# Spreading a three-hop graph kernel's softmax over its gather steps and moving all of its dense rows beside the first hop's scatters

## The chip, the cores and the metric

The kernel runs on one core of one Trainium2 chip. The metric is the device time of one execution in microseconds (us), lower is better. TensorE is called PE, VectorE DVE, ScalarE ACT, GpSimd POOL, and SyncE SP; SP computes nothing here and issues most of the DMAs.

## The reference

There are 50,000 rows of 128 floats (`x`), and 25,000 edges with a source row (`head`, in the code's terms), a destination row (`tail`) and one of 64 types. `h` is the layer norm of `x` with a ReLU. Three times ("hops") this is done, starting from `agg = h`:

```
left = agg[head] @ q_w;  right = tanh((rel * agg[tail]) @ k_w);  att = sum(left * right, axis=1)
w = softmax of att over the edges that have the same head
agg = segment_sum(w * rel * agg[tail], head) / max(count, 1), then each row divided by its norm
out = out + agg + h
```

The result is `x + out`. Rows that are no edge's head have an aggregate of zero, so for them the result is `x + 3 h`. That is the "dense part": it is done for all rows, and the rows that have edges are overwritten at the end.

## The kernel before, in words

The kernel first sorts the edges by head. Then it works on 200 tiles of 125 edges, in 50 groups of 4 tiles (`NG`, `GT`), and the groups form four chunks of 13, 13, 13 and 11 groups (`GC`). Each hop has the same shape.

**Gather steps.** POOL issues one indirect DMA for each tile of a group (`fetch`, L599; in hop 0 two, for tail and head) into a ring of `TS` = 5 groups. For each group DVE multiplies the gathered rows with the relation rows (`product`, L1065), PE transposes (`turn`, L1351), multiplies with `kw` (`keys`, L1358) and with `qw` (`back`, L1371 and L1373), ACT copies and takes the tanh, and DVE forms the scores three steps later (`scores`, L1088). Hop 0 has 29 steps of two groups (a few of one), and a layer norm in each; hops 1 and 2 have 53 steps of one group. A ring place is free for the next fetch once `product` has run, and in hop 0 also once the row that was gathered for the head has been stored to `acc_d`.

**Softmax of a chunk.** When the scores of a chunk are there (steps in `SOFT_AT`), DVE runs `softmax(h, b)` in one piece: seven times it asks PE for a small transpose, or ACT for the exponential, and waits for the answer (`to_pe`, L951 to L971). PE then multiplies each tile with its weights for the rows that cross from tile to tile (`parts`, L1399), `PARTS` tiles a step, and `carries` gives the carried rows to SP, which writes them into `rt` (`s_cy`).

**Sums.** For a group j of a finished chunk, DVE makes the weights (`weights`, L1003), PE forms the segment sums (L1416), ACT squares and copies them (L1239, L1241), and six groups later DVE scales them (`scale`, L1023; in hop 2 L1029 to L1033, with three rows from memory that SP loads with `load_last`). Every fifth group there is `norms` (L1011 to L1018). During the gather steps a sum is done in each step (in hop 2 every other step) as soon as chunks are ready; what is left runs behind the last gather step, after the softmax of the last chunk: groups 17 to 49 in hop 0, 32 to 49 in hop 1, 16 to 49 in hop 2.

**Between the hops.** After the gathers of hop 0 POOL issues 200 indirect DMAs that scatter the scaled sums to `ntab_d` (L611, one per tile, each group after its `scale`), and only when all have landed does it gather from there for hop 1. Hop 1 stores its groups to `agg_d` through SP, and hop 2 gathers from there when all are stored. At the end POOL scatters hop 2's groups to the output (L611).

**Dense part.** 26,624 rows are done in hop 0's first 13 steps. The others are `ND` = 23 chunks of 1,024 rows. `dense_at` says where: 8 with the sums 22, 25, ..., 43 of hop 0, 7 in the steps 0, 3, ..., 18 of hop 1, and 8 in the steps 0, 3, ..., 21 of hop 2. Each is a load by SP (`load_x`, L462) into one of two buffers in `hr`, statistics and layer norm on DVE (`dense_in`, L725 and L703 to L718), ReLU on ACT into `hd` (L1190), one addition on DVE (`dense_out`, L731) and a store by SP (`store_out`, L468). SP waits for the store of a buffer before it loads into it again.

Every engine's order is written out by hand, and all waiting is on semaphores, so an engine that waits holds up whatever stands behind in its order.

Of the kernel before, what the change touches and what calls it, by code (L numbers as in the profile page):

```python
# [42 lines left out]
DC = 8  # L43
DROWS = P * DC
# [21 lines left out]
SOFT_AT = [[[g in u for u in UNITS].index(True) + 2 for g in (GC[c + 1] - 1 for c in range(LAST))],  # L66
           [GC[c + 1] + 2 for c in range(LAST)], [GC[c + 1] + 2 for c in range(LAST)]]
PARTS = [26, 18, 18]
COUNTS_AT = [2 + c for c in range(K)]
EVERY = [1, 1, 2]  # L70
CARRY_AT = [[SOFT_AT[h][c] + (h > 0) + -(-CT[c] // PARTS[h]) + 1 for c in range(LAST)] for h in range(HOPS)]


def parts_at(h, s):

    for c in range(LAST):
        n = (s - SOFT_AT[h][c] - (h > 0)) * PARTS[h]
        if 0 <= n < CT[c]:
            return c, range(n, min(n + PARTS[h], CT[c]))
    return 0, range(0)  # L80


def sums_by_step(h):
    steps, j = [], 0
    for s in range(STEPS[h]):
        ready = max([0] + [GC[c + 1] for c in range(LAST) if s >= CARRY_AT[h][c]])
# [12 lines left out]

def sums_left(h):  # L100

    return range(SUMS[h][-1].stop, GC[LAST])


def parts_left(h, j):

    left = sums_left(h)
    each = -(-CT[LAST] // len(left))
    n = j - left.start
    return range(min(n * each, CT[LAST]), min((n + 1) * each, CT[LAST]))  # L110


def gnn_kernel(nc, x, src, dst, etype, edge_emb, q_w, k_w, out):
    ctx = ExitStack()
    with ctx:  # L115
# [289 lines left out]
        def _(sp):  # L405
# [64 lines left out]
            def dense(what, h, s, back):  # L470
                if (what, h, s - back) in dense_at:
                    store_out(dense_at[what, h, s - back])
                if (what, h, s) in dense_at:
                    load_x(dense_at[what, h, s] + 1)
# [24 lines left out]
            def sums(h, j):  # L499
# [3 lines left out]
                else:  # L503
                    if j >= LAG:
                        store_agg(h, j - LAG)
                    dense("sums", h, j, 1)

            for h in range(HOPS):
# [19 lines left out]
                for s in range(STEPS[h]):  # L528
# [15 lines left out]
                    else:  # L544
                        load_agg(s + 2)
                        load_rel(s + 4)
                        dense("edges", h, s, 2)
# [12 lines left out]
                for j in sums_left(h):  # L560
                    sums(h, j)
                carries(h, LAST)
                for j in range(GC[LAST], NG):
                    sums(h, j)
                if h < HOPS - 1:
                    for g in range(NG - LAG, NG):
                        store_agg(h, g)
                else:
# [92 lines left out]
        def _(dve):  # L661
# [60 lines left out]
            def dense_in(c, between=()):  # L722
# [4 lines left out]
                layer_norm(dstats, dlns, DC, s_dln, between)  # L727
# [5 lines left out]
            def dense(what, h, s, back, between=()):  # L733
                if (what, h, s - back) in dense_at:
                    dense_out(dense_at[what, h, s - back])
                if (what, h, s) in dense_at:
                    dense_in(dense_at[what, h, s], between)
                else:
                    for work in between:
                        work()  # L740
# [77 lines left out]
            def to_pe():  # L818
                dve.sem_inc(s_seg, 1)
                segs[0] += 1  # L820
                dve.wait_ge(s_segp, segs[0])
            pads = ((LL, PADKEY), (LF, 0.0), (LB, 0.0), (LSP, 0.0))
# [70 lines left out]
            def whole_segments(add, b, state):  # L893


                op0, op1 = (ALU.mult, ALU.add) if add else (ALU.add, ALU.max)
                n, part = CT[b], slice(TC[b], TC[b + 1])
                GFt, GBt = (gf[0:n, b, :], gb[0:n, b, :]) if add else (gfn[0:n, b, :], gbn[0:n, b, :])
                x, xf, xb, f, back = (t[0:n, :] for t in (seg_x, seg_xf, seg_xb, seg_f, seg_b))
                rg, rgn, rwf, rwb = (rows[:, k, part] for k in ((G_, GN, WGF, WGB) if add else (GNEG, GNNEG, WGFN, WGBN)))  # L900
                none = 0.0 if add else LOWEST
# [9 lines left out]
                to_pe()  # L911
# [4 lines left out]
                to_pe()  # L916
# [9 lines left out]
            def to_columns(dest, b):  # L926
# [558 lines left out]
```

## Time and profile before

| | |
|---|---|
| median of 3 runs | 2115.43 us (2114.66 to 2116.12) |
| the profiled execution's own time | 2108.43 us |
| its span | 2106.6 us |
| DVE busy | 64% |
| POOL busy | 59% |
| PE, its weight loads | 52%, 42% |
| ACT busy | 40% |
| mean granted TensorE clock | 0.683 of full speed |

A row of a group of instructions has line, engine, operation, output and inputs, and count. In a row of a timeline the first number is the start in us from the span's start, the second the length; what follows in brackets is the idle time of the engine ahead of it, and who ended it. Shares of busy time are means over stages that have different limits.

### The profile page before, as it was taken

To read this page: it belongs to the slowest core of one execution; us is meant where nothing else is said; L and a number is where in the kernel's file an instruction comes from. 1 tells how busy PE (TensorE), PEld (TensorE's weight loads), DVE (VectorE), ACT (ScalarE), POOL (GpSimd) and SP (SyncE) were. 2 spreads that over 40 slices of the span, in tenths; PEclk is the share of its full clock that TensorE was granted. 3 is DMA by queue.
4 is the path that set the end of the run, shared out by engine and by line. 5 is a ranking of instruction groups with operands and counts; after the bars stand their busy time and mean duration, and the time that the engine had idled before them with its cause. 6 is when DMAs were issued, how large, how long until landed. Compare 5 with 4: busy or idle time off the path is not lost. (4 is left out here: it accounts for less than half of the span.)

```text
span 2106.6 us, 23618 instructions
## 1 busy us (share of the span) xinstructions
PE 1085.6 (52%) x5196; PEld 878.5 (42%) x5196; DVE 1358.1 (64%) x6127; ACT 842.2 (40%) x2649; POOL 1233.6 (59%) x1218
## 2 busy tenths in 40 slices
PE   0111354375586585653036769668355874756420
PEld 0001233263374474642024557557233763645410
DVE  8897688667656747885036575775546655579870
ACT  2221567646635544664023244444332422234420
POOL 1002777657757757777777665600474556567776
PEclk9999856556666656655568677785676867665555
DMA  8802555544324323445146455521697779457771
GB/s 234 239 27 95 190 171 195 174 145 141 118 81 118 104 90 112 166 159 177 40 130 211 141 145 138 160 79 72 159 161 176 162 140 192 116 141 209 208 202 35
DMA packets 199662, 302.96 MB, mean 144 GB/s; under 512 B 31696, under 2 KB 113948, under 8 KB 196064
## 3 DMA queue, kind: packets, MB, share of 16 engines
q1 hardware_dynamic: 161120, 228.46, 34.1%
q0 software_dynamic: 38400, 72.99, 17.0%
q8 instruction: 43, 0.70, 0.1%
q14 instruction: 99, 0.81, 0.1%
HBM read 175.89 MB, written 130.86 MB: 146 GB/s over the span
## 5 line engine op out<-in xcount | busy, mean ns | idle before, releaser
L599 POOL DMA_INDIRECT tr<-in_x_dram,tidx x200 | 200.1, 1000 | 315.6 <-DVEq L838 183.9
L599 POOL DMA_INDIRECT tr<-agg_d,tidx x200 | 196.4, 982 | 252.5 <-issue 184.7
L1416 PE MATMUL ps<-rt,wr 128*125 128x128 f32 x1200 | 255.1, 381 | 172.5 <-DVE wr L1003 121.3
L1351 PE MATMUL ps<-ident,rt 128*128 128x128 f32 x600 | 135.0, 367 | 361.2 <-DVE rt L1065 298.7
L1416 PEld LDWEIGHTS ps<-rt,wr 128*125 128x125 f32 x1200 | 223.9, 279 | 188.1 <-DVE wr L1003 132.9
L1198 ACT COPY rtT<-ps 128x512 f32<-128x512 f32 x150 | 88.3, 589 | 514.0 <-PE ps L1351 513.5
L1239 ACT ACTIVATE sqj<-ps,invc 125x128 bf16<-125x128 f32 x600 | 212.5, 373 | 177.4 <-PE ps L1416 177.2
L599 POOL DMA_INDIRECT tr<-ntab_d,tidx x200 | 200.9, 1004 | 104.5 <-issue 61.5
L1351 PEld LDWEIGHTS ps<-ident,rt 128*128 128x128 f32 x600 | 95.0, 189 | 386.0 <-DVE rt L1065 314.8
L611 POOL DMA_INDIRECT out_dram<-rt,lidx x200 | 210.8, 1054 | 69.7 <-issue 60.6
L611 POOL DMA_INDIRECT ntab_d<-rt,lidx x200 | 210.2, 1051 | 60.8 <-issue 60.2
L599 POOL DMA_INDIRECT xr<-in_x_dram,hidx x200 | 207.7, 1039 | 60.9 <-issue 58.5
L1358 PE MATMUL ps<-rtT,kw 128*128 128x512 f32 x300 | 234.6, 877 | 7.9 <-ACT rtT L1198 7.9
L1065 DVE TENSOR_TENSOR rt<-tr,relr 128x512 f32<-128x512 f32 x150 | 101.2, 688 | 190.4 <-ACT hr L1190 151.0
L1399 PEld LDWEIGHTS ps<-wfl,rt 128*128 128x128 f32 x1200 | 208.7, 269 | 1.3 <-DVE wfl L971 0.8
L1399 PE MATMUL ps<-wfl,rt 128*128 128x2 f32 x1200 | 203.6, 300 | 0.7 <-DVE wfl L971 0.7
L1003 DVE TENSOR_SCALAR wr<-segbc,lcol,wcol 128x125 f32<-128x125 uint8 x600 | 167.1, 356 | 14.6 <-PE ps L1416 14.2
L1371 PEld LDWEIGHTS ps<-qwT,thT 128*128 128x128 f32 x624 | 107.3, 239 | 75.2 <-issue 56.5
L1204 ACT ACTIVATE thT<-ps 128x512 f32<-128x512 f32 x150 | 89.9, 599 | 111.9 <-PE ps L1358 110.5
L1239 ACT ACTIVATION_READ_ACCUMULATOR sqj<-ps,invc 125x1 f32 x600 | 126.9, 211 | 0.0
L1088 DVE SCALAR_TENSOR_TENSOR junk<-ps,xr 128x128 bf16<-128x128 f32 x400 | 98.4, 282 | 42.2 <-PE ps L1373 42.1
L1373 PEld LDWEIGHTS ps<-qwT,thT 128*128 128x128 f32 x576 | 98.4, 251 | 42.2 <-issue 40.5
(229 smaller groups left out, 2264.3 us busy)
## 6 DMA issues: line engine op xcount, KB each, us to landing
agg_d<-rt SPq DMA_DIRECT2D x100, 258.0 KB
xr<-agg_d SPq DMA_DIRECT2D x100, 258.0 KB, 3.9
relr<-rel_d SPq DMA_DIRECT2D x100, 256.0 KB, 5.0
ntab_d<-rt SPq DMA_DIRECT2D x15, 1679.7 KB
rt<-in_x_dram SPq DMA_DIRECT2D x13, 1024.0 KB, 6.5
out_dram<-rt SPq DMA_DIRECT2D x13, 1024.0 KB, 4.1
acc_d<-xr SPq DMA_DIRECT2D x50, 258.0 KB, 3.1
rel_d<-relr SPq DMA_DIRECT2D x50, 256.0 KB, 3.5
```

Of the source, the lines that this page charges most:

```text
L599: G.indirect_dma_start(out=row, out_offset=None, in_=table[:, :], in_offset=bass.IndirectOffsetOnAxis(ap=idx[:, n:n + 1], axis=0)).then_in ...
L611: G.indirect_dma_start(out=table[:, :], out_offset=bass.IndirectOffsetOnAxis(ap=lidx[:, n:n + 1], axis=0), in_=rt[:, n, 0:width], in_offse ...
L1003: ins = V.tensor_scalar(wr[:, (j % 2) * GT + t, 0:R], segbc[:, n, :], lcol[:, n:n + 1], wcol[:, n:n + 1], ALU.is_equal, ALU.mult)
L1065: V.tensor_tensor(edge_rows(g), ring(tr, g, TS), ring(relr, g, RS), ALU.mult).then_inc(s_rt, 1)
L1088: ins = V.scalar_tensor_tensor(junk[:, t, :], z, 1.0, left[:, (g % n) * GT + t, 0:D], ALU.mult, ALU.mult, accum_out=att[:, g * GT + t:g * ...
L1239: A.activation(sqj[0:R, t, :], ps[B_T + j % 2][0:R, t, :], ACT.Square, scale=invc[0:R, n:n + 1], accum_out=ssq[0:R, j // NB % 2, k:k + 1]) ...
L1351: ins = T.transpose(ps[B_TR][:, t, :], rt[:, g * GT + t, 0:D], ident[:, :])
L1358: T.matmul(bank(B_KW), kw[:, :], flat2(rtT[:, (g % 2) * GT:(g % 2 + 1) * GT, :]), start=True, stop=True).then_inc(s_rg, 1)
L1371: ins = T.matmul(z, th, qwT[:, :], start=True, stop=True)
L1373: ins = T.matmul(ps[B_Z + g % 2][:, t, :], th, qwT[:, 0:D], start=True, stop=True)
L1399: ins = T.matmul(bank(B_S)[:, 2 * n:2 * n + 2], rt[:, TC[b] + n, 0:D], wfl[:, n, :], start=True, stop=True)
L1416: ins = T.matmul(ps[B_T + j % 2][0:R, t, :], wr[:, (j % 2) * GT + t, 0:R], rt[:, j * GT + t, 0:D], start=True, stop=True)
```

## The change

Softmax is cut into eight stages (`softmax(h, b, stage)`), a stage ending where DVE would wait for PE or ACT: `ask` at the end of one and `answered` at the start of the next. During the gather steps they stand at three places of a step in hop 0 (ahead of the types, ahead of the statistics, behind the layer norm) and at two in hops 1 and 2 (behind `product`, behind `scores`), in DVE's, PE's and ACT's order alike. So a chunk's softmax takes parts of four steps in hop 0 and of five in hops 1 and 2. `parts` comes behind the last stage, 13 tiles a step instead of 18 in hops 1 and 2, in four steps instead of three. The first sum of a hop comes 3 steps later in hop 0 (step 14 for 11), and 4 later in hops 1 and 2 (24 for 20), so that 36, 22 and 36 sums are left behind the last step instead of 33, 18 and 34.

Behind the last step five of the left sums (`FILL`) stand between the stages of the last chunk's softmax, and two (`HOLD`) behind `carries`, ahead of the sums of the last chunk. The `parts` of the last chunk are divided among those in between: 18, 4 and 18 sums, where it was 22, 7 and 23.

All 23 dense chunks stand in hop 0: one with each of the sums 27 to 45, and four (`TAIL`) behind the last `scale` of hop 0, ahead of hop 1's first step. The core of the diff:

```
+STAGES = 8
+PLACES = [3, 2, 2]
+READY_AT = [... as SOFT_AT before ...]
-PARTS = [26, 18, 18]
+PARTS = [26, 13, 13]
+STAGE_AT = [{(READY_AT[h][c] + place(h, i)[0], place(h, i)[1]): (c, i) for c in range(LAST) for i in range(STAGES)}
+            for h in range(HOPS)]
+PARTS_AT = [[READY_AT[h][c] + place(h, STAGES - 1)[0] for c in range(LAST)] for h in range(HOPS)]
+CARRY_AT = [[PARTS_AT[h][c] - (-CT[c] // PARTS[h]) for c in range(LAST)] for h in range(HOPS)]
+FILL, HOLD = 5, 2
...
-        for k in range(8):
-            dense_at["sums", 0, 22 + 3 * k] = next(chunks)
-        for h, n in ((1, 7), (2, 8)):
-            for k in range(n):
-                dense_at["edges", h, 3 * k] = next(chunks)
+        for j in range(NG - ND, NG - TAIL):
+            dense_at["sums", 0, j] = next(chunks)
+        for k in range(TAIL):
+            dense_at["tail", 0, k] = next(chunks)
...
+            def dense(what, h, s):
+                c = dense_at.get((what, h, s))
+                if c is not None:
+                    if c > 0:
+                        dense_out(c - 1)
+                    dense_in(c)
...
                     else:
                         if s < NG:
                             product(h, s)
-                        dense("edges", h, s, 2, scores(h, s - 3) if s >= 3 else ())
+                        softmax(h, *stage_at(h, s, 0))
+                        if s >= 3:
+                            for work in scores(h, s - 3):
+                                work()
+                        softmax(h, *stage_at(h, s, 1))
...
-                softmax(h, LAST)
-                for j in sums_left(h):
+                for i in range(STAGES):
+                    softmax(h, LAST, i)
+                    for j in sum_behind(h, i):
+                        sums(h, j)
+                for j in sums_mixed(h):
                     sums(h, j)
                 carries(h, LAST)
-                for j in range(GC[LAST], NG):
+                for j in (*sums_held(h), *range(GC[LAST], NG)):
                     sums(h, j)
...
+                if h == 0:
+                    for k in range(TAIL):
+                        dense("tail", 0, k)
+                    dense_out(ND - 1)
```

## Rows read from the trace of the kernel before

**Rows 1.** The page's chain that ended last, by engine

```profile
POOL 7%; issue 3%; DVE 1%; POOLq 0%; PE 0%; ACT 0%; DVEq 0%
```

**Rows 2.** POOL's indirect DMAs by line, duration min/median/max, first and last start

```profile
L599 POOL DMA_INDIRECT tr<-ntab_d,tidx x200: 938/944/2058, 1065.9 to 1368.1; - x100
L599 POOL DMA_INDIRECT tr<-agg_d,tidx x200: 939/945/1587, 1496.6 to 1816.9; - x100
...
L611 POOL DMA_INDIRECT ntab_d<-rt,lidx x200: 982/982/2167, 792.5 to 1062.7; - x100
L611 POOL DMA_INDIRECT out_dram<-rt,lidx x200: 982/983/2575, 1818.2 to 2097.5; - x100
```

**Rows 3.** POOL's waits in hops 0, 1, 2: us in total, times, longest

```profile
POOL tr L599 <- DMA acc_d<-xr: 69.4, 13, 13.5
POOL tr L599 <- DVE rt L1065: 43.1, 10, 8.6
POOL tr L599 <- DVE rt L1065: 67.8, 16, 13.2
```

**Rows 4.** DVE's timeline in hop 0's scatters: last softmax, first left sums

```profile
830.07 0.28 DVE L951 COPY seg_x<-ps 44x125 f32<-44x125 f32 x1 [0.44 <-PE ps L1386]
...
842.30 1.10 DVE L1003 TENSOR_SCALAR wr<-segbc,lcol,wcol 128x125 f32<-128x125 uint8 x4
...
843.92 1.10 DVE L1003 TENSOR_SCALAR wr<-segbc,lcol,wcol 128x125 f32<-128x125 uint8 x4
...
855.16 1.10 DVE L1003 TENSOR_SCALAR wr<-segbc,lcol,wcol 128x125 f32<-128x125 uint8 x4
```

**Rows 5.** The same timeline: one dense chunk, then the last four sums

```profile
897.79 1.64 DVE L725 BATCH_NORM_STATS2 stats<-hr 128x6 f32<-128x128 f32 x8
...
902.54 1.12 DVE L1003 TENSOR_SCALAR wr<-segbc,lcol,wcol 128x125 f32<-128x125 uint8 x4
...
905.87 1.23 DVE L731 SCALAR_TENSOR_TENSOR hr<-ohT,hr 128x1024 f32<-128x1024 f32 x1 [1.61 <-ACT ohT L1190]
...
964.66 1.10 DVE L1003 TENSOR_SCALAR wr<-segbc,lcol,wcol 128x125 f32<-128x125 uint8 x4
...
983.52 0.15 DVE L1159 COPY ucol<-ps 128x1 f32<-128x1 f32 x1
```

**Rows 6.** The page's DMA issues: the dense chunks, median us to landing last

```profile
hr<-in_x_dram SPq DMA_DIRECT2D x23, 512.0 KB, 5.0
out_dram<-hr SPq DMA_DIRECT2D x23, 512.0 KB, 4.4
```

**Rows 7.** Windows, scatters alone: us, POOL busy (x), clock, DMA share, GB/s

```profile
860.00:983.00 123.00, 96.18 (x89) 0.56 0.49 167
983.00:1064.00 81.00, 61.78 (x63) 0.50 0.23 75
```

**Rows 8.** `product`, first and last start: hop 1's steps 0, 28, 41 on, hop 2's first

```profile
L1065 DVE TENSOR_TENSOR rt<-tr,relr x15: 678/684/716, 1072.4 to 1149.0; 128x512 f32<-128x512 f32 x15
L1065 DVE TENSOR_TENSOR rt<-tr,relr x13: 673/682/686, 1241.0 to 1328.5; 128x512 f32<-128x512 f32 x13
L1065 DVE TENSOR_TENSOR rt<-tr,relr x9: 680/685/686, 1331.8 to 1397.3; 128x512 f32<-128x512 f32 x9
L1065 DVE TENSOR_TENSOR rt<-tr,relr x15: 685/692/757, 1506.3 to 1595.5; 128x512 f32<-128x512 f32 x15
```

**Rows 9.** PE's timeline in hop 1: a step with 18 parts, later sums

```profile
1264.67 5.40 PE L1399 MATMUL ps<-wfl,rt 128*128 128x2 f32 x36
1269.93 2.05 PE L1416 MATMUL ps<-rt,wr 128*125 128x128 f32 x8
...
1275.17 5.43 PE L1399 MATMUL ps<-wfl,rt 128*128 128x2 f32 x36
...
1295.51 1.04 PE L1416 MATMUL ps<-rt,wr 128*125 128x128 f32 x8
```

**Rows 10.** The page's groups: the score of one tile | busy us, mean ns

```profile
L1088 DVE SCALAR_TENSOR_TENSOR junk<-ps,xr 128x128 bf16<-128x128 f32 x400 | 98.4, 282 | 42.2 <-PE ps L1373 42.1
```

More of the change, by code:

```diff
@@ L43 @@
 DC = 8
+TAIL = 4
 DROWS = P * DC
@@ L85, in sums_by_step @@
     for s in range(STEPS[h]):
-        ready = max([0] + [GC[c + 1] for c in range(LAST) if s >= CARRY_AT[h][c]])
+        ready = max([0] + [GC[c + 1] for c in range(LAST) if s > CARRY_AT[h][c]])
         n = int(j < ready and s % EVERY[h] == 0 and s < STEPS[h] - 1)
@@ L97, in sums_at, with sums_mixed, sums_held, sum_behind @@
     return SUMS[h][s] if 0 <= s < STEPS[h] else range(0)
+FILL, HOLD = 5, 2
 def sums_left(h):
     return range(SUMS[h][-1].stop, GC[LAST])
+def sums_mixed(h):
+    return sums_left(h)[FILL:len(sums_left(h)) - HOLD]
+def sums_held(h):
+    return sums_left(h)[-HOLD:]
+def sum_behind(h, i):
+    return sums_left(h)[i:i + 1] if i < FILL else range(0)
 def parts_left(h, j):
-    left = sums_left(h)
-    each = -(-CT[LAST] // len(left))
-    n = j - left.start
+    mixed = sums_mixed(h)
+    each = -(-CT[LAST] // len(mixed))
+    n = j - mixed.start
     return range(min(n * each, CT[LAST]), min((n + 1) * each, CT[LAST]))
@@ L505, in sums @@
                         store_agg(h, j - LAG)
-                    dense("sums", h, j, 1)
+                    dense("sums", h, j)
             for h in range(HOPS):
@@ L720, in layer_norm, with dense_in @@
                     work()
-            def dense_in(c, between=()):
+            def dense_in(c):
                 dve.wait_ge(s_xd[c % 2], 16 * (c // 2 + 1))
@@ L731, in dense_out, with dense @@
                 V.scalar_tensor_tensor(flat2(xd[c % 2]), flat2(hd), 3.0, flat2(xd[c % 2]), ALU.mult, ALU.add).then_inc(s_do, 1)
[L733 to L740, printed above, removed]
+            def dense(what, h, s):
+                c = dense_at.get((what, h, s))
+                if c is not None:
+                    if c > 0:
+                        dense_out(c - 1)
+                    dense_in(c)
             dve.wait_ge(s_const, 11)
@@ L915, in whole_segments, with by_edge @@
                 ch(V.tensor_tensor(rcar[1][:, 0:n - 1], rgn[:, 0:n - 1], rscan[1][:, 1:n], op0))
-                to_pe()
+            def by_edge(add, b):
+                n, (op0, op1), none, (GFt, GBt), _ = terms(add, b)
+                x, xf, xb, f, back = (t[0:n, :] for t in (seg_x, seg_xf, seg_xb, seg_f, seg_b))
                 car = bank(B_S)[0:n, S_CAR:S_CAR + 2]
@@ L1040, in sums @@
                     scale(h, j - LAG)
-                dense("sums", h, j, 1)
+                dense("sums", h, j)
             def early_out(c):
@@ L1153, in _ @@
                     scale(h, j)
+                if h == 0:
+                    for k in range(TAIL):
+                        dense("tail", 0, k)
+                    dense_out(ND - 1)
                 if h < HOPS - 1:
@@ L1436, in _ @@
                             turn(h, s)
+                        softmax(*stage_at(h, s, 0))
                         if 1 <= s <= NG:
@@ L1446, in _ @@
                     if h == 0 and s in COUNTS_AT:
-                        whole_segments(COUNTS_AT.index(s))
+                        ends(COUNTS_AT.index(s))
+                        over_tiles(COUNTS_AT.index(s))
                         to_columns(COUNTS_AT.index(s))
-                softmax(LAST)
-                for j in sums_left(h):
+                for i in range(STAGES):
+                    softmax(LAST, i)
+                    for j in sum_behind(h, i):
+                        sums(h, j)
+                for j in sums_mixed(h):
                     parts(h, LAST, parts_left(h, j))
@@ L1453, in _ @@
                 carries(LAST)
-                for j in range(GC[LAST], NG):
+                for j in (*sums_held(h), *range(GC[LAST], NG)):
                     sums(h, j)
```

187 lines of the change are left out of this document (118 added, 69 removed).

## Prediction, made before the changed kernel ran

> **What bounds the kernel now.** I read the page first. The busy shares name no engine, and the chain at its end [rows 1] is short, but it says that the end is POOL issuing scatters. So I listed POOL's indirect DMAs by line [rows 2]. They divide the run: gathers of hop 0 until the scatters begin at 792.5, these until 1062.7, hop 1's gathers 1065.9 to 1368.1, hop 2's 1496.6 to 1816.9, the last scatters to 2097.5. Only between 1368 and 1497 has POOL nothing to issue: there hop 1's tail runs on PE, ACT and DVE. A change pays only if it shortens one of these stretches, so POOL's waits come next [rows 3]: 69 us in hop 0 for rows to be stored, which is `product`'s step being late, 43 us in hop 1 and 68 us in hop 2 for `product` itself. These are about the most that the gathers can give. The scatter stretch of hop 0 has no such loss: 200 scatters go back to back, 1.35 us each [rows 2]. After that I went through DVE's timeline in the first scatter stretch [rows 4, 5], as everything that the change adds there is DVE's, and PE's in the steps with `parts` [rows 9].
>
> **The scatter stretch of hop 0.** Before, DVE is through its last `scale` at 983.5 [rows 5] and POOL goes on for 79 us from work that is ready. The change puts 15 more dense chunks here. A chunk alone takes 897.79 to 902.54 for statistics and layer norm, 3.3 us until ACT's part is through (DVE has one sum's weights and scale meanwhile, then waits 1.6), and 1.15 for the addition (the next instruction overlaps its end): 9.2 us from one `dense_in` to the next if one follows each sum [rows 5]. POOL wants a group each (1063.7 - 792.5) / 50 = 5.4 us [rows 2]. So DVE falls back by 3.8 us with each of 19 groups, and the question is what lead it has.
>
> The last softmax starts at 829.7 and ends at 842.3 [rows 4]. With five sums in it at 1.62 us each (842.30 to 843.92), one `norms` of 2.7, and some 3 us of its waits filled, it takes 20 us. Eight sums follow without dense work; five took 12.9 before (842.30 to 855.16), 2.6 each, and with three `parts` rather than two ahead of each I take 2.8, so 22 us. Sum 27 starts at 872, and its scale of group 21 comes well ahead of POOL, which wants that group at 792.5 + 21 x 5.4 = 906. The lead of 34 us is used up after nine groups. 19 rounds of 9.2, less 2.8 for the first one's missing addition, three `norms` that outlast the wait (0.9 each) and `carries` (3.6) give 178 us: the last `dense_in` ends at 1050. Group 40 is scaled at 1054, and POOL then needs ten groups at 5.4, and 2.2 us to the first gather: 1111 instead of 1065.9, **+45**. The last four sums (18.9 us, 964.66 to 983.52) keep ahead of it. The four tail chunks start at 1069 and end after 4 x 9.2 + 1.2, at 1107, before the first gathered rows land at some 1117: no cost, but little cover; in a slower DVE order each us of theirs beyond 10 would show.
>
> A buffer must be stored and loaded again within one round: 4.4 + 5.0 us in the medians over all dense chunks, and 0.9 for the two issues, is 10.3 against 9.2 [rows 6]. These medians are over all 23 chunks, those of hops 1 and 2 too, where each step has two other loads beside them. I add 5 us, with bounds of nothing and 35: **+50**.
>
> One row speaks of POOL itself: with DVE busy beside it a scatter came each 123 / 89 = 1.38 us, with DVE idle each 81 / 63 = 1.29 [rows 7]. [...]
>
> **Gathers of hop 0.** The softmax lump of 12.6 us held up three steps. In pieces, the seven waits go, and stages behind the layer norm lie in DVE's wait for ACT. But the two others of a step lengthen the way to the layer norm, by some 3 us a step, and the 26 `parts` of a step stay and only come three steps later, for the last chunk at POOL's end. Of POOL's 69 us in 13 waits [rows 3], the longest 13.5, I give a third to steps without softmax. I take **-15**, between 0 and -35.
>
> **Hop 1.** The lump is 13 us and `parts` three steps of 10.5 us each [rows 9]; 13 steps take 90.8 us (1241.0 to 1331.8) and POOL alone would need 13 x 5.1 = 67 [rows 8, 2]. After: four softmax steps, in which DVE has 3.9 us of its own (`product` 0.7, four scores 1.1, a sum 1.6, a fifth of `norms` 0.5) [rows 8, 10, 4] plus a quarter of 10 us, 6.4 each, 26 us; four steps with 13 `parts`, 13 x 0.30 for these and 5.2 for PE's other work, 9.1 each, 36 us [rows 9]; five of 3.9 and `carries` 3.6, 23 us. That is 85, as DVE and PE take turns, so -6, and with some overlap -9. The chunk before has no sums now until step 24, so POOL's pace of 5.4 holds in its softmax steps: -14. The last nine steps have the same lump: -5. The first 15 lose dense chunks that POOL was mostly hiding: -2. Together **-30**; bounds -10 (PE as now, no overlap) and -55 (43 us of POOL's waits, and a shorter lag of `product` behind it).
>
> Hop 1's tail: four more left sums at 2.4 to 2.8 us, +10; five of them in the softmax's pauses and two beneath the landing of the carried rows save 5. **+5**, -3 to +12.
>
> **Hop 2.** From the first to the 15th `product` it is 89.2 us (1506.3 to 1595.5) where hop 1 has 76.6 [rows 8]; the DMA engines also carry five dense chunks of 0.5 MB in and 0.5 MB out each there [rows 6]. Hop 1 carries the same five without harm, so they aren't the whole of the 12.6 us; I give them two thirds: -8. The others much as in hop 1: -8, -11, -6. **-33** at POOL's end of gathers, between -20 and -62 (POOL's waits are 68). The last scatters are POOL's in either case, with ready groups at their start: 0, -9 to +10.
>
> **Sum.** -15 + 50 - 30 + 5 - 33 = **-23 us**. The profiled execution had 2108.4 us, its span 2106.6; the median of the runs is 7 us above it. I take the difference off the median: 2092 us.
>
> **Rivals.** (1) PE keeps its upper clock level. In the steps with `parts` a sum takes 2.05 us, and shortly after them 1.04 [rows 9]: PE comes out of the lump, during which it idles, at 1.2 GHz and works through `parts` at that level. In stages PE is never idle that long. At the upper level a step with `parts` is about 3 us shorter; 24 steps give 72 us, of which POOL's waits leave some 30. With the sum's other terms as they are, that is 2062 us. The Trainium skill (TensorE: Matmul & The Clock Gate, HAM oscillation) says that gaps without work throttle the array; the rows agree, but they also show the low level in the middle of dense `parts`. Against this rival: `parts` ran at that level long after PE was busy again, and they are still there. Chance 0.24.
>
> (2) On the other side: the two buffers set the pace of the dense chunks. If store and load take 11.3 us instead of 9.2, as the medians nearly say, 19 rounds cost 40 us rather than my 5: 2092 + 35 = 2127. It decides from a round of 10.7 us, (23 + 5) / 19 above 9.2. Each such wait also holds SP, behind which the stores of hop 0's groups stand, though nothing early needs these. Chance 0.12.
>
> (3) The gathers give little: the lump was only moved, since PE's in-order queue now waits in each softmax step for DVE's next stage, ahead of `keys`, and `parts` takes four low-clock steps. With -8 and -18 in place of -30 and -33 the sum is +14: 2129 us. The POOL waits and the lump's 13 us speak against it. Chance 0.12.
>
> My case has 0.52, from 2073 to 2113. With the rivals, the range is 2050 to 2123. Differences under 0.2% (4 us) can hardly be told from no change. Faster 0.75 (the first rival and all but a little of my case), the same 0.05, slower 0.20.
>
> **What would show it.** The gathers of hop 1 begin near 1096 (1111 less 15), DVE's dense additions lie about 9.3 us apart, and POOL waits for DVE between scatters for the first time. Hop 1's gathers take some 275 to 285 us instead of 302, hop 2's some 287 instead of 320. I am wrong if the rounds are longer than 10 us, if the last `product` of hops 1 and 2 doesn't come nearer to their first, or if the granted clock in the steps with `parts` is at the upper level.

## The result, and the profile after

| kernel | median, us | lowest to highest | runs |
|---|---|---|---|
| before | 2115.05 | 2112.21 to 2116.12 | 4 |
| after | 2058.88 | 2044.53 to 2070.04 | 4 |

The ratio is 0.973 with an interval of [0.967, 0.979]: 56 us faster. The four runs of after lie in two pairs, 2045 and 2049, 2069 and 2070. The profiled execution is of the faster pair: it has 2049.01 us, its span is 2046.8, and its mean granted clock is 0.688 (0.683 before).

The page's chain that ended last, by engine, in the kernel after:

```profile
POOL 7%; issue 3%; DVE 3%; PE 2%; POOLq 0%; DMA 0%; SPq 0%; DVEq 0%
```

It again tells only of the end. POOL's indirect DMAs by line, after (durations min/median/max, first and last start), answer to [rows 2]:

```profile
L638 POOL DMA_INDIRECT tr<-ntab_d,tidx x200: 940/944/1733, 1094.9 to 1355.9; - x100
L638 POOL DMA_INDIRECT tr<-agg_d,tidx x200: 940/944/1535, 1488.0 to 1755.6; - x100
...
L650 POOL DMA_INDIRECT ntab_d<-rt,lidx x200: 980/982/1953, 762.2 to 1087.7; - x100
L650 POOL DMA_INDIRECT out_dram<-rt,lidx x200: 980/982/2581, 1756.9 to 2037.7; - x100
```

The starts divide the span as those of before did; the gathers of hop 0 are counted from the first one for a head (193.3 and 193.8). "Hop 1" here goes from its first `product` to its last, and "tail" from there to hop 2's first gather. The last column is the prediction's term.

| stretch, us | before | after | difference | predicted |
|---|---|---|---|---|
| gathers of hop 0 | 599.2 | 568.4 | -30.8 | -15 |
| scatters of hop 0 | 273.4 | 332.7 | +59.3 | +50 |
| hop 1 | 324.9 | 272.0 | -52.9 | -30 |
| tail of hop 1 | 99.3 | 114.6 | +15.3 | +5 |
| gathers of hop 2 | 321.6 | 268.9 | -52.7 | -33 |
| last scatters, to the end | 288.4 | 289.9 | +1.5 | 0 |
| span | 2106.6 | 2046.8 | -59.8 | -23 |

**Where the 59 us come from.** POOL's groups by line, first of before, then of after (busy us, mean ns of one | idle before them and who ended it):

```profile
L611 POOL DMA_INDIRECT ntab_d<-rt,lidx x200 | 210.2, 1051 | 60.8 <-issue 60.2 <-DVE rt L1065 0.3 <-DMA ntab_d<-rt,lidx 0.3
L599 POOL DMA_INDIRECT tr<-ntab_d,tidx x200 | 200.9, 1004 | 104.5 <-issue 61.5 <-DVE rt L1065 43.1
```

```profile
L650 POOL DMA_INDIRECT ntab_d<-rt,lidx x200 | 211.1, 1055 | 115.4 <-issue 64.6 <-DVE rt L1103 50.7
L638 POOL DMA_INDIRECT tr<-ntab_d,tidx x200 | 201.8, 1009 | 66.8 <-issue 66.8
L638 POOL DMA_INDIRECT tr<-agg_d,tidx x200 | 194.8, 974 | 204.5 <-issue 189.9 <-DVE rt L1145 14.5
```

In the scatters POOL now waits 50.7 us for `scale` (L1103), where it waited for nothing. The 200 scatters themselves cost (211.1 + 64.6) / 200 = 1.38 us each rather than 1.35, 5 us together, and the last one is followed by 7.2 us to the first gather rather than 3.2. That is 50.7 + 5 + 4, the whole difference of 59.3. In hop 1 the 43.1 us of waits for `product` are gone, in hop 2 14.5 are left of 67.8 [rows 3].

DVE's timeline after, at the start of the last softmax, at the first dense chunk, at two dense additions, at the last one and at hop 1's first work:

```profile
808.05 0.28 DVE L1011 COPY seg_x<-ps 44x125 f32<-44x125 f32 x1
...
854.43 1.64 DVE L764 BATCH_NORM_STATS2 stats<-hr 128x6 f32<-128x128 f32 x8
...
900.51 1.23 DVE L770 SCALAR_TENSOR_TENSOR hr<-ohT,hr 128x1024 f32<-128x1024 f32 x1 [1.60 <-ACT ohT L1282]
...
909.74 1.23 DVE L770 SCALAR_TENSOR_TENSOR hr<-ohT,hr 128x1024 f32<-128x1024 f32 x1 [1.62 <-ACT ohT L1282]
...
1084.05 1.22 DVE L770 SCALAR_TENSOR_TENSOR hr<-ohT,hr 128x1024 f32<-128x1024 f32 x1 [3.25 <-ACT ohT L1282]
...
1101.31 0.17 DVE L1144 CAST tidx<-tr 128x4 int32<-128x4 f32 x1 [13.75 <-DMA tr<-ntab_d,tidx]
```

POOL's timeline: a stall at the start of the scatters, the first one in the dense rounds, and a later one:

```profile
806.30 0.98 POOL L650 DMA_INDIRECT ntab_d<-rt,lidx  x1 [6.66 <-DVE rt L1103]
...
927.43 0.98 POOL L650 DMA_INDIRECT ntab_d<-rt,lidx  x1 [2.61 <-DVE rt L1103]
...
974.74 0.98 POOL L650 DMA_INDIRECT ntab_d<-rt,lidx  x1 [3.79 <-DVE rt L1103]
```

Additions come 909.74 - 900.51 = 9.23 us apart (10.1 in a round with `norms`), and POOL loses 3.8 us in a round like the last one shown. The tail chunks are over at 1085.3; DVE then stands 13.75 us until hop 1's rows land. The page's issues of the dense chunks (median us to landing last) answer to [rows 6]:

```profile
hr<-in_x_dram SPq DMA_DIRECT2D x23, 512.0 KB, 3.9
out_dram<-hr SPq DMA_DIRECT2D x23, 512.0 KB, 2.7
```

With every chunk in hop 0's scatters and behind them, store and load take 2.7 + 3.9 us in place of 4.4 + 5.0.

**Where the gathers gain.** From one `product` to another, us between the starts of the steps 0, 14, 28, 41, 49:

| | 0 to 14 | 14 to 28 | 28 to 41 | 41 to 49 |
|---|---|---|---|---|
| hop 1 before | 76.6 | 92.0 | 90.8 | 65.5 |
| hop 1 after | 73.7 | 71.6 | 79.6 | 47.2 |
| predicted difference, and measured | -2, -2.9 | -14, -20.4 | -9, -11.2 | -5, -18.3 |
| hop 2 before | 89.2 | 85.0 | 100.8 | 68.3 |
| hop 2 after | 73.5 | 79.1 | 82.1 | 50.9 |
| predicted difference, and measured | -8, -15.7 | -8, -5.9 | -11, -18.7 | -6, -17.4 |

The windows of hop 1's steps 28 to 41 and 41 to 49, before and after (us, busy of PE, PEld, DVE, ACT, POOL with counts, granted clock, DMA share, GB/s):

```profile
1241.00:1331.80 90.80, 71.42 (x407) 60.30 (x406) 59.21 (x302) 39.60 (x147) 53.51 (x54) 0.74 0.55 153
1331.80:1397.30 65.50, 46.61 (x292) 39.52 (x291) 41.74 (x203) 23.96 (x89) 22.30 (x23) 0.77 0.42 119
```

```profile
1246.72:1326.28 79.56, 68.20 (x421) 56.61 (x419) 60.31 (x313) 42.19 (x155) 61.27 (x61) 0.85 0.63 174
1326.28:1373.43 47.15, 40.47 (x236) 34.18 (x236) 37.64 (x183) 21.64 (x79) 24.33 (x23) 0.82 0.56 152
```

The counts of steps 28 to 41 are as before and a little higher; PE's granted clock rose from 0.74 to 0.85, and PE's busy time fell by 3.2 us. The other 8 us are pauses that are gone. `parts` in the last three steps with a burst before hop 1's last `product`, PE's timeline after (it answers to [rows 9]):

```profile
1353.68 3.98 PE L1505 MATMUL ps<-wfl,rt 128*128 128x2 f32 x26
...
1363.06 3.00 PE L1505 MATMUL ps<-wfl,rt 128*128 128x2 f32 x26
...
1370.69 2.96 PE L1505 MATMUL ps<-wfl,rt 128*128 128x2 f32 x26
```

13 tiles take 3.0 us in two of them, 0.23 each; in [rows 9] 18 took 5.4, 0.30 each. The windows of single bursts say what differs: the granted clock. First a burst of before (that of [rows 9]), then four in a row of after and one more (us, PE busy with count, granted clock, DMA share, GB/s):

```profile
1264.67:1270.07 5.40, 5.40 (x36) 0.75 0.78 224
```

```profile
1279.11:1282.17 3.06, 3.06 (x26) 1.00 0.85 232
1285.18:1288.14 2.96, 2.96 (x26) 1.00 0.44 90
1291.15:1294.11 2.96, 2.96 (x26) 1.00 0.42 84
1298.79:1302.32 3.53, 3.53 (x26) 0.81 0.53 120
...
1626.97:1632.55 5.58, 5.55 (x26) 0.50 1.02 126
```

The last row is the one burst of after (in hop 2) that lies wholly at the lower level: 5.55 us for 13 tiles, 0.43 each. Up to the last `product` of each hop, 19 of the 23 bursts of after have a granted clock of 0.93 or more, and 4 of the 18 of before.

### The profile page after: what moved, and what is told of

Same layout as the page of the kernel before. It is cut to its first block and busy times, and to the rows that moved or that the text cites. A ratio compares the mean times of both kernels' runs of the same rounds, so it can differ in the third digit from the quotient of the medians.

```text
span 2046.8 us, 23618 instructions
## 1 busy us (share of the span) xinstructions
PE 1100.0 (54%) x5196; PEld 874.6 (43%) x5196; DVE 1364.2 (67%) x6127; ACT 846.4 (41%) x2649; POOL 1234.4 (60%) x1218
## 5 line engine op out<-in xcount | busy, mean ns | idle before, releaser
L1522 PE MATMUL ps<-rt,wr 128*125 128x128 f32 x1200 | 267.3, 393 | 240.2 <-DVE wr L1083 217.6
L1522 PEld LDWEIGHTS ps<-rt,wr 128*125 128x125 f32 x1200 | 232.0, 288 | 262.4 <-DVE wr L1083 236.0
L650 POOL DMA_INDIRECT ntab_d<-rt,lidx x200 | 211.1, 1055 | 115.4 <-issue 64.6
L638 POOL DMA_INDIRECT xr<-in_x_dram,hidx x200 | 202.9, 1015 | 61.0 <-issue 59.1
L1505 PEld LDWEIGHTS ps<-wfl,rt 128*128 128x128 f32 x1200 | 190.8, 250 | 0.5
L1505 PE MATMUL ps<-wfl,rt 128*128 128x2 f32 x1200 | 187.0, 288 | 0.0
L1282 ACT ACTIVATE ohT<-hr,lns 128x128 f32<-128x128 f32 x184 | 73.3, 480 | 105.0 <-DVE lns L757 105.0
```

The source lines that it names most:

```text
L638: G.indirect_dma_start(out=row, out_offset=None, in_=table[:, :], in_offset=bass.IndirectOffsetOnAxis(ap=idx[:, n:n + 1], axis=0)).then_in ...
L650: G.indirect_dma_start(out=table[:, :], out_offset=bass.IndirectOffsetOnAxis(ap=lidx[:, n:n + 1], axis=0), in_=rt[:, n, 0:width], in_offse ...
L1505: ins = T.matmul(bank(B_S)[:, 2 * n:2 * n + 2], rt[:, TC[b] + n, 0:D], wfl[:, n, :], start=True, stop=True)
L1522: ins = T.matmul(ps[B_T + j % 2][0:R, t, :], wr[:, (j % 2) * GT + t, 0:R], rt[:, j * GT + t, 0:D], start=True, stop=True)
```

## The experiments

One thing has to be known first. The chips on which the experiments ran took 2509 to 2568 us for the kernel before, 19 to 21% more than the first chip, with the same code. So each is compared with the kernel before of its own call, and stretch by stretch with `before_again` (the kernel before, not edited); what that slowness is follows in the last section. Two profiles of one kernel on two of these chips (the `_2` runs) differ by up to 6 us in hop 1 and in the gathers of hop 2, 10 in the scatters, 13 in the gathers of hop 0 and 17 in the last stretch; a profiled execution lies up to 24 us from the median of its kernel (`before_again`: 2532.7). `before_again` was profiled on the chip of `after_again`, so a stretch of another run set against these two has the difference of the chips in it.

| run | median, us | ratio to before, interval | gathers 0 | scatters 0 | hop 1 | tail 1 | gathers 2 | last |
|---|---|---|---|---|---|---|---|---|
| before_again | 2508.8 | 0.998 [0.994, 1.003] | 772.8 | 346.1 | 398.1 | 99.4 | 372.0 | 342.4 |
| after_again | 2519.3 | 0.999 [0.992, 1.005] | 793.2 | 403.8 | 347.5 | 114.5 | 333.1 | 339.6 |
| stages_only | 2467.0 | 0.982 [0.975, 0.988] | 765.7 | 328.5 | 360.9 | 114.6 | 337.5 | 342.0 |
| stages_only_2 | 2459.0 | 0.980 [0.971, 0.989] | 778.9 | 335.9 | 366.4 | 114.7 | 338.8 | 324.9 |
| dense_only | 2581.9 | 1.026 [1.020, 1.032] | 763.5 | 397.1 | 394.6 | 99.1 | 376.2 | 346.0 |
| dense_only_2 | 2574.1 | 1.018 [1.010, 1.026] | 773.9 | 391.6 | 400.4 | 99.1 | 377.3 | 347.4 |
| hybrid | 2457.3 | 0.971 [0.963, 0.978] | 771.0 | 337.0 | 357.4 | 117.9 | 336.7 | 336.7 |
| hybrid_2 | 2464.1 | 0.979 [0.972, 0.986] | 768.7 | 346.9 | 359.4 | 114.7 | 330.5 | 337.4 |
| hybrid_parts9 | 2471.7 | 0.963 [0.957, 0.968] | 786.1 | 346.9 | 349.3 | 114.0 | 338.4 | 330.9 |
| parts18 | 2551.3 | 1.013 [1.003, 1.022] | 782.3 | 408.9 | 382.5 | 102.2 | 344.4 | 338.2 |
| lump_parts13 | 2561.8 | 0.997 [0.994, 1.001] | 800.9 | 333.3 | 407.2 | 100.2 | 376.1 | 340.8 |
| warm_lump | 2550.0 | 1.016 [1.008, 1.023] | 746.6 | 334.6 | 419.3 | 99.3 | 384.3 | 355.4 |

### The two halves of the change, each alone

`stages_only` is the kernel after with the dense chunks where they were before:

```
-        for j in range(NG - ND, NG - TAIL):
-            dense_at["sums", 0, j] = next(chunks)
-        for k in range(TAIL):
-            dense_at["tail", 0, k] = next(chunks)
+        for k in range(8):
+            dense_at["sums", 0, 22 + 3 * k] = next(chunks)
+        for h, n in ((1, 7), (2, 8)):
+            for k in range(n):
+                dense_at["edges", h, 3 * k] = next(chunks)
... the calls that serve these places, on SP, DVE and ACT
```

`dense_only` is the kernel before with the same lines the other way round. Both ran again as `stages_only_2` and `dense_only_2`, on another chip.

> The changed kernel with its dense chunks put back where they were before (8 with sums 22 to 43 of hop 0, 7 and 8 in the steps of hops 1 and 2). If the shorter gathers come from the softmax in stages, hop 0's scatter stretch is back at 273 us (from 333), hop 1's product runs from first to last in 275 to 285 us and hop 2's gathers take 280 to 295, and the time is 2020 to 2040 us. If they come from the dense chunks having left (rival), hop 1 keeps some 310 us and hop 2 some 310, and the time is 2070 to 2085 us.

> The kernel before with nothing changed but the place of the dense chunks: 19 with sums 27 to 45 of hop 0 and four behind its last scale. The softmax is in one piece. If the stages make the gathers short, hop 0's scatter stretch grows by 45 to 55 us, hop 1's gathers gain 0 to 5 and hop 2's 8 to 20, and the time is 2135 to 2155 us, slower than before. If the dense chunks' leaving makes them short (rival), the gathers give back 60 us or more and the time is 2095 to 2110 us.

> stages_only once more, since all kernels of its call, the one before too, took some 19% longer than in the measurement of the change. If the stages carry the gain, hop 0's scatter stretch is about 273 us, hop 1's product takes 275 to 285 us from first to last, hop 2's gathers 280 to 295, time 2020 to 2040 us where the kernel before takes 2115. Rival (the dense chunks' leaving carries it): 2070 to 2085 us.

> dense_only once more, for the same reason. If the stages carry the gain: scatter stretch 45 to 60 us longer, hop 1's gathers 0 to 5 us shorter, hop 2's 8 to 20, time 2135 to 2155 us. Rival: 2095 to 2110 us.

Measured: the stages alone give 2% (0.982 and 0.980), the move of the dense chunks alone costs 2% (1.026 and 1.018). The directions are those expected; the stages were expected to give 4%, and their gain is smaller on these chips. The stretches say where. In `dense_only` the scatters of hop 0 take 392 to 397 us for 346, and hops 1 and 2, freed of 15 chunks, gain nothing: 395 to 400 for 398, 376 to 377 for 372. In `stages_only` hop 1 has 361 to 366 for 398 and hop 2 338 for 372, with all their chunks in place. Only beside the stages does the move give something back: `after_again` has 347.5 and 333.1, so some 16 us in hop 1 and 5 in hop 2, against the 68 to 75 that its scatters of hop 0 take longer than `stages_only`'s. With the softmax in one piece (the lump), a dense chunk in a step cost nothing that these runs show. That holds for the steps ahead of the first lump too: from step 0 to 14 hop 1 takes 106.6 and 102.9 us in `dense_only` and its repeat, without the five chunks, and 101.5 in `before_again`; hop 2 takes 102.3 and 102.7 there, and 95.2.

### The same pair on a third chip

`after_again` and `before_again` are the two kernels, unedited.

> The changed kernel itself, unedited, as a control beside the experiments, whose calls ran on chips where the kernel before takes 2515 to 2522 us. If the two parts of the change simply add, stages_only (ratio 0.980) and dense_only (1.018 to 1.026) make a ratio of 1.00 here, and the stretches are: hop 0's scatters 395 to 410 us, hop 1's product 350 to 360 from first to last, hop 2's gathers 325 to 335. If the two help each other (rival: stages and the empty gathers only pay together), the ratio is 0.975 as on the chip of the first measurement. Beside parts18 (ratio 1.013) it tells what 13 tiles of parts a step are worth: below 1.00 says 13 matter.

> The kernel before, unedited, for a profile from the same chip as after_again. If the stages shorten the gathers here as they did in the first measurement, its stretches are: hop 1's product 405 to 420 us from first to last, hop 2's gathers 380 to 395, hop 0's scatters 328 to 337. If this chip's slowness lies where neither the lump nor the dense chunks are (rival), hop 1's product takes less than 390 us.

Measured: 0.999 for after, no change, where the first chip had 0.973. The stretches of `after_again` less `before_again` are +20, +58, -51, +15, -39, -3, and the two halves add up to it (0.981 x 1.022 = 1.003). Scatters, hop 1 and its tail differ as on the first chip (+59, -53, +15). What differs is the gathers of hop 0 (+20 for -31) and those of hop 2 (-39 for -53). So the forecast gain of 1% is not there on a chip of this sort, while the added scatter time and the shorter hop 1 are seen on both. The ratio of 1.00 was expected, from adding up the halves; the three stretches expected of `before_again` were all missed (hop 1 398 for 405 to 420, hop 2 372 for 380 to 395, scatters 346 for 328 to 337).

### Fewer chunks beside the scatters

`hybrid` is `stages_only` with 14 chunks beside every second sum of hop 0, 5 in hop 1 and 4 in hop 2, so that POOL's lead of 34 us, as the prediction has it, isn't used up.

```
-        for k in range(8):
-            dense_at["sums", 0, 22 + 3 * k] = next(chunks)
-        for h, n in ((1, 7), (2, 8)):
+        for k in range(14):
+            dense_at["sums", 0, 18 + 2 * k] = next(chunks)
+        for h, n in ((1, 5), (2, 4)):
```

The minus lines are those of `stages_only`.

> The changed kernel with 14 dense chunks in hop 0, one with every second sum from 18 to 44, and nine where POOL sets the pace and no sums run yet: five in hop 1 (steps 0, 3, ..., 12) and four in hop 2 (steps 0, 3, 6, 9). A pair of sums with one chunk takes DVE 11.3 us or less and POOL wants 10.8, so the scatter stretch should be 273 to 285 us instead of 333; hop 1's gathers should lose 0 to 3 us and hop 2's 3 to 8: 2000 to 2015 us. If the DMA traffic of the dense chunks is what made the gathers of hops 1 and 2 long (rival), they lose 20 us or more there and the time is 2030 us or above.

> hybrid once more, for the same reason: scatter stretch 273 to 285 us, hop 1's gathers 0 to 3 us longer than in the changed kernel, hop 2's 3 to 8, time 2000 to 2015 us. Rival (the dense chunks' traffic made the gathers long): 2030 us or above.

Measured: 0.971 and 0.979, and the scatters are back at 337 and 347 us (346 in `before_again`). Hops 1 and 2 keep what they had in after to within 12 us. So the 59 us come from DVE's rounds with one chunk per sum, as the prediction has it, and 14 chunks at every second sum all but take them away: beside `stages_only` of the same chips the scatters take 8 and 11 us more. POOL's groups by line in `after_again`, then in `hybrid`:

```profile
L650 POOL DMA_INDIRECT ntab_d<-rt,lidx x200 | 213.7, 1069 | 185.5 <-DVE rt L1103 123.0 <-issue 62.6
L638 POOL DMA_INDIRECT tr<-ntab_d,tidx x200 | 196.1, 981 | 139.8 <-DVE rt L1145 76.0 <-issue 63.7
```

```profile
L647 POOL DMA_INDIRECT ntab_d<-rt,lidx x200 | 210.1, 1050 | 124.6 <-DVE rt L1102 62.6 <-issue 62.0
...
L635 POOL DMA_INDIRECT tr<-ntab_d,tidx x200 | 195.6, 978 | 148.0 <-DVE rt L1144 86.3 <-issue 60.4 <-remote 1.3
```

The wait for `scale` halves (123.0 to 62.6 us; `before_again` has 40.1), and the one for `product` grows by 10. It is faster than before on both chips it ran on, by 2 to 3%, where after is level with before on a third. But most or all of that is the stages: beside `stages_only` of its own chips it has 2457 us for 2467 and 2464 for 2459, which is no difference. That moving any dense chunk pays is not shown. It missed the expected 2000 to 2015 us (5% below before), and it didn't run on the first chip.

### PE kept busy in the lump

`warm_lump` is the kernel before with small products that nobody reads in PE's `softmax`, in the first three chunks of hops 1 and 2. It adds PE work, and leaves out none.

```
+            def spin(n):
+                for _ in range(n if warm[0] else 0):
+                    T.matmul(bank(B_KW)[:, 0:40], kw[:, :], kw[:, 0:40], start=True, stop=True)
```

Five stand behind the first answer, 3 and 12 behind each pair of answers, 3 at the end, and PE waits for ACT's tanh (`s_th`) ahead of the first.

> The kernel before with one thing added: in hops 1 and 2 PE does small products that nobody reads between its answers in the softmax of the first three chunks, so it is not idle in the lump. DVE's lump stays as long. If PE's low clock behind the lump is what made the gathers long, sums in the steps with parts take near 1.1 us instead of 2.05, the granted clock of hop 1's gathers rises from 0.75 towards 0.85, and each hop's gathers get 15 to 30 us shorter: 2065 to 2090 us. If it is DVE's 13 us in one piece (rival), the clock may rise but the gathers gain less than 8 us each: 2100 to 2118 us.

Measured: slower by 1.6%, hop 1 21 us and hop 2 12 us longer. Windows of hop 1, `before_again`, then `warm_lump`:

```profile
1312.50:1702.50 390.00, 241.13 (x1185) 193.48 (x1186) 193.15 (x1030) 121.31 (x375) 198.22 (x200) 0.68 0.45 128
```

```profile
1274.60:1684.70 410.10, 282.19 (x1402) 234.94 (x1403) 192.30 (x1023) 119.94 (x368) 197.14 (x200) 0.68 0.43 122
```

PE is busy 41 us longer and its granted clock is 0.68 in both. The lumps themselves, hop 1's second, from the copy of the first answer to the end of the softmax, PE alone, `before_again`, then `warm_lump`:

```profile
1537.20:1549.89 12.69, 1.50 (x9) 0.50 0.12 33
```

```profile
1505.45:1522.82 17.37, 15.30 (x73) 0.51 0.07 19
```

PE was busy for 15.3 us of 17.4 instead of 1.5 of 12.7, and the clock stayed at the lower level. The added products also stood on the path: the six lumps of hops 1 and 2 take 16 to 18 us instead of 12 to 13, together 13 us more in hop 1 and 14 in hop 2, of the 21 and 12 by which the hops are longer. So what was to be tested did not come about: the lump did not stay as long, and the clock did not rise. The run shows that this work in PE's pauses doesn't raise it; it can't say what a raised clock would give. The Trainium skill (TensorE: Matmul & The Clock Gate, HAM oscillation) would have the array sped up by closing the gaps; this run does not show it.

### The size of a burst of `parts`, with stages and with the lump

`parts18` is the kernel after with `PARTS = [26, 18, 18]`, `lump_parts13` the kernel before with `PARTS = [26, 13, 13]`.

> The changed kernel with 18 tiles of parts a step in hops 1 and 2 as before (three steps instead of four, carries and the first sums one step earlier). If the number a step is indifferent, as PE's total is the same, the time is within 5 us of the changed kernel's 2059. If 13 matter (rival), since the longer bursts hold product's step beyond what the ring of five groups covers, hops 1 and 2 lose 5 to 10 us each: 2069 to 2079 us.

> The kernel before (softmax in one piece, dense chunks where they were) with 13 tiles of parts a step instead of 18 in hops 1 and 2. parts18 took 382 us from hop 1's first product to its last where after_again took 348. If small bursts of parts are worth that by themselves, this kernel has some 370 us there instead of before_again's 398, and hop 2's gathers shrink from 372 to 360: ratio 0.985 or lower. If they are only worth it together with the stages (rival), since behind a lump of 13 us POOL's ring has run out anyway, hop 1 stays above 390 and the ratio is 0.995 to 1.005.

Measured: with 18 tiles hop 1 takes 382.5 us for 347.5, its tail 102.2 for 114.5 and hop 2 344.4 for 333.1, together 34 us, and the ratios (1.013 and 0.999) differ by as much; 5 to 10 us a hop were expected. With the lump, 13 tiles give nothing: 407.2 for 398.1, 376.1 for 372.0, and the ratio is 0.997 [0.994, 1.001]. The products of the parts, two for each tile, over all hops (min/median/max ns), in `before_again` and `after_again`:

```profile
L1399 PE MATMUL ps<-wfl,rt x1200: 164/352/374, 482.9 to 2405.4; 128*128 128x2 f32 x172
```

```profile
L1505 PE MATMUL ps<-wfl,rt x1200: 164/251/374, 578.5 to 2366.8; 128*128 128x2 f32 x172
```

These medians are of a mixture. Taken one by one, the products that ran wholly at the upper level have a median of 251 ns and those at the lower level 352 or 353 in every run, so the median of all jumps when the share at the upper level passes one half (`parts18` has 352, `lump_parts13` 301). What the runs differ in is that share. In the gather steps, of the products recorded there:

| | first chip: before | first chip: after | before_again | lump_parts13 | parts18 | after_again |
|---|---|---|---|---|---|---|
| lump or stages, tiles a burst | lump, 18 | stages, 13 | lump, 18 | lump, 13 | stages, 18 | stages, 13 |
| at the upper level, hop 1 | 66% | 91% | 54% | 84% | 61% | 84% |
| at the upper level, hop 2 | 73% | 86% | 59% | 55% | 40% | 67% |

The level goes with the size of the burst and not with the stages. The twelve profiles of these chips fit that, though in hop 2 the two sizes overlap: with 18 tiles (five profiles, one of them with stages) 54 to 65% in hop 1 and 40 to 60% in hop 2, with 13 (six, one of them with the lump) 70 to 88% and 55 to 77%, with 9 (one) 80% and 75%. `lump_parts13` shows that a higher level gives no time by itself: hop 1 has 84% there, as in `after_again`, and is no shorter than before. Most of the time came where both the lump and the long bursts were gone.

### Smaller bursts still

`hybrid_parts9` is `hybrid` with `PARTS = [26, 9, 9]`.

> hybrid with 9 tiles of parts a step in hops 1 and 2 (six steps instead of four, so carries and the first sums come two steps later and more sums are left). If PE's bursts are what the gathers still wait for, hop 1's product goes from 359 to 345 us and hop 2's gathers from 331 to 322; the tail of hop 1 gets 5 to 8 us longer: ratio 0.970 against hybrid's 0.971 to 0.979. If 13 is small enough already (rival), only the tail's cost is left and the ratio is 0.978 to 0.985.

Measured: 0.963 [0.957, 0.968], the lowest ratio of all. Its stretches are those of `hybrid` within what repeats differ by (hop 1 -8 to -10, hop 2 +2 to +8), and `hybrid` didn't run beside it. So that nine tiles beat 13 is not shown. It is 3.7% faster than before, where after is level with before on a chip of that sort.

## Why the prediction was right, and where its sum was off

The forecast was 2092 us in a range of 2050 to 2123, and the median is 2059: faster, as said, and 33 us below the figure. It lies outside the likeliest case's own 2073 to 2113 and at the first rival's 2062, and the gain of 56 us is more than twice the 23 forecast. That the range was met is in part luck: the gathers of hop 0 gave 16 us more than their term for a reason that stays open, and nothing of it on the other chips, where after is level with before.

**The scatters of hop 0 went as described.** The round was computed at 9.2 us and is 9.23; the lead was to last nine groups, and the first stall comes at 927.4, 73 us or eight rounds after the first dense chunk (854.4); hop 1's gathers were due at 1096 and begin at 1094.9 (1101 with the 5 us that the sum adds for the buffers). The tail chunks are hidden, with 13.75 us of cover rather than 10. The split is off: POOL's gathers ended 30 us earlier, but the last softmax starts only 22 us earlier (808.05 against 830.07), so 8 us passed from one term to the other (most of it is the stall of 6.66 us at 806). Together they make +28.5, predicted +35. The rows that show scatters 1.38 us apart with DVE busy and 1.29 with DVE idle [rows 7] have no term in the sum. The scatters came 1.38 us apart over the whole stretch for 1.35, 5 us in all; whether that is DVE's doing is not shown, since the DMA share differs between the two windows too (0.49 and 0.23).

**Rival (2) fell.** Rounds of 9.23 us are below its 10.7, and store and load together take 6.6 us where all chunks run without edge transfers beside them. The step that feared it used medians over all chunks, those of hops 1 and 2 too.

**Hops 1 and 2 gave more: the sizes of two terms failed.** The larger one is the step with `parts`, put at 9.1 us. The bursts of after begin 6.0 to 9.4 us apart, 7.2 on average over 17 distances (10.5 at [rows 9], 9.7 on average in before). Over 24 steps that would be some 46 us, an estimate from these distances, and the two hops gave 43 us more than forecast. In steps 28 to 41 the total came close (-11.2 for -9) although this term was too long there (6.1, 6.0 and 7.6 us apart): other steps were longer than their 3.9 and 6.4 us. The step "the last nine steps have the same lump: -5" failed: -18.3 and -17.4. Part of this is no gain. In the last nine steps the third chunk's `parts` and `carries` now fall at the end and pass into the tail, and the tail has +15.3 for +5. Taken together, last nine steps and tail of hop 1 are -3.0 against a forecast of 0. `parts18` agrees: it has the tail back at 102.2 us, and its last nine steps take 83.5 us for 59.7 in `after_again`. DVE's timeline in hop 1's tail after:

```profile
1379.65 0.16 DVE L1060 TENSOR_TENSOR scF<-s_half,ps 128x1 f32<-128x1 f32 x1 [1.86 <-PE ps L1505]
...
1384.71 0.42 DVE L1074 COPY fxr<-ps 52x256 f32<-52x256 f32 x1 [3.94 <-PE ps L1512]
...
1396.84 0.27 DVE L1011 COPY seg_x<-ps 44x125 f32<-44x125 f32 x1
```

`carries` of chunk three runs 6 to 11 us after the last `product` at 1373.4, and the last softmax starts only at 1396.8, 23 us after it (before 13: 1409.9 and 1397.3). The other term is hop 2's first 14 steps, with a gain of two thirds of 12.6 us for the dense chunks that left: -15.7 for -8, and hop 2 now has 73.5 there where hop 1 has 73.7. That the chunks were the cause is not shown: on the other chips these steps take 95.2 us with them (`before_again`) and 102 to 103 without (`dense_only`, `dense_only_2`, `after_again`).

**Gathers of hop 0: -31 for -15 on the first chip, +20 on the third.** The bounds were 0 and -35. `stages_only` and `stages_only_2` have 766 and 779 us against 773, `after_again`, whose edits in that stretch are the same, 793. So the stages of hop 0 can't be told from nothing there. What may hide them are pauses of DVE that the profile ascribes to no releaser of this core (`remote`). In hop 0's gathers they add up to 75 to 82 us in the five profiles of kernels with the lump on these chips and to 153 to 177 in the seven with stages, and neither profile of the first chip has any. DVE's longest such waits there, `before_again`, then `after_again` (us, times, longest):

```profile
DVE lns L715 <- remote: 15.2, 6, 3.5
```

```profile
DVE lns L742 <- remote: 32.8, 6, 8.8
```

Why the stages have twice as much of them is open, and so is what made -31 on the first chip: no run there undoes them.

**Rival (1): its effect came, its cause is not borne out.** It had 3 us less per step with `parts` because PE would keep the upper level, not idling in the lump. The clock did rise, from 0.75 to 0.82 between hop 1's first and last `product` and from 0.72 to 0.76 over hop 2's gathers, and most bursts ran at the upper level (19 of 23 for 4 of 18), so a burst of 13 took 3.0 to 3.1 us in most steps where the forecast had 13 x 0.30 = 3.9, and PE's other work was shorter too: the sum behind the burst at 1285.2 takes 1.12 us, where [rows 9] has 2.05. The prediction's third sign of being wrong, the upper level in the steps with `parts`, is there. The step that failed is the term of 9.1 us, which took 0.30 us a tile for the price at the low level: that burst had a granted clock of 0.75, a tile at the lower level takes 0.43 us (5.55 / 13) and one at the upper 0.23. As for the cause, `lump_parts13` keeps PE idle in the lump and has 84% of its part products at the upper level in hop 1, `parts18` has the stages and 61%. So shorter bursts went with the level, and not the missing lump; why is open. `warm_lump` can't decide on the pauses, as the clock didn't rise in it.

**Rival (3) fell** on both sorts of chip: hop 1 gave -53 and -51, hop 2 -53 and -39, against its -8 and -18.

## What to carry to other kernels

When work is moved to a place where another engine is the bound, compute the time of a round there with the moved work, and how long the lead lasts; that sum held to 0.1 us a round, and it also shows the spacing (`hybrid`) at which the lead is hardly spent. Test each half of a change alone: here, on chips of the second sort, one gave 2% and the other cost 2%, and moving work out of a stretch pays nothing where it was hidden. A long wait and a long burst in one step are worth cutting together: with the lump, shorter bursts gave nothing, and with the long bursts, stages alone gave less. Don't price work by a duration without the granted clock beside it, and don't read a median of products that ran at two levels as a change of the product.

## What the runs showed of the hardware

**The same kernel, 20% slower on other chips.** The kernel before took 2115 us on the first chip and 2509 to 2568 on four others. The sort (first gather at 191.4 and 191.6) and the tail of hop 1 (99.3 and 99.4 us) are the same to 0.5 us. Longer are the stretches with POOL's indirect DMAs, whose own durations are not (medians of 944 and 947 ns in hop 1). POOL's waits in hop 0 in `before_again`, which answer to [rows 3], and the indirect gathers of hop 1 by line:

```profile
POOL tr L599 <- DMA acc_d<-xr: 227.2, 14, 27.4
```

```profile
L599 POOL DMA_INDIRECT tr<-ntab_d,tidx x200: 942/947/2058, 1312.5 to 1682.5; - x100
```

DVE's timeline in `before_again`, layer norm beside the last scores of hop 0:

```profile
1000.24 0.17 DVE L710 TENSOR_SCALAR lns<-lns 128x16 int32<-128x16 int32 x1 [3.83 <-remote]
...
1007.94 0.17 DVE L715 TENSOR_TENSOR lns<-lns 128x16 f32<-128x16 f32 x1 [3.11 <-remote]
...
1012.14 0.17 DVE L716 SCALAR_TENSOR_TENSOR lns<-lns 128x16 f32<-128x16 f32 x1 [3.82 <-remote]
1012.23 0.28 DVE L1088 SCALAR_TENSOR_TENSOR junk<-ps,hr 128x128 bf16<-128x128 f32 x1
...
1013.55 0.17 DVE L714 SCALAR_TENSOR_TENSOR lns<-lns 128x16 f32<-128x16 f32 x1 [1.02 <-DVE lns L716]
1013.76 0.17 DVE L715 TENSOR_TENSOR lns<-lns 128x16 f32<-128x16 f32 x1
1013.96 0.17 DVE L716 SCALAR_TENSOR_TENSOR lns<-lns 128x16 f32<-128x16 f32 x1
```

In one chain of DVE instructions that feed each other, some come 0.2 us apart and some 3 to 4 us, with no releaser that the profile can name (`remote`). These stand just behind the gathers of hop 0; within them such pauses of DVE come to 76 us. POOL's waits grew by 158 us, so they may be a part of the cause; that they are all of it is not shown. It looks like instructions that come late, but no run here separates that from other causes, so it stays open.

**The part products and the clock.** One such product (128 rows by 128, two columns, float32) takes 251 ns in the median at the upper level and 352 at the lower, and a burst of 13 tiles 2.96 and 5.55 us (after). In `warm_lump` PE was busy for 15.3 of 17.4 us in a lump, and the granted clock was 0.51.

**Two levels of one kernel on one chip.** Four runs of after gave 2045, 2049, 2069 and 2070 us, four of before 2112 to 2116. The cause is open; 20 us is more than several terms of the sum, and a third of the gain.
